# A second PSUM bank for the rounded copies, and new instruction orders on VectorE and ScalarE, in layer 0 of a two-layer graph network

## What is computed

```python
agg = jax.ops.segment_sum(x[src], dst, num_segments=N)
h = (1.0 + eps) * x + agg
h = jax.nn.relu(batch_norm(h @ W1 + b1, g1, be1))   # W1: 512 x 1024, layer 0
h = h @ W2 + b2                                     # W2: 1024 x 512
...
# layer 1: where(indeg > 0, agg, x) @ W.T + b, relu, batch norm
```

## Time and profile before

| | |
|---|---|
| median of 3 runs | 2925.01 us (2919.75 to 2929.12) |
| the profiled execution's own time | 2951.29 us |
| its span | 2949.5 us |
| mean granted TensorE clock | 0.902 |
| busy, share of the span | PE 81%, PEld 54%, DVE 49%, ACT 35%, POOL 53% |
| layer 0, from the second pair's start to the 25th's | 93.6 to 1218.2 us |

### The profile page before, as it was taken

The page is one execution under the profiler, slowest core; times in us unless marked ns, Lnnn a source line. Parts: engine busy times, 40 slices in busy tenths (PEclk is TensorE's granted clock), DMA queues, the critical chain, the costliest instruction groups (busy, mean ns, idle before and its releaser), DMA issues. The chain is left out here.

```text
span 2949.5 us, 42174 instructions
## 1 busy us (share of the span) xinstructions
PE 2402.7 (81%) x9711; PEld 1593.3 (54%) x9712; DVE 1447.7 (49%) x2269; ACT 1022.3 (35%) x1776; POOL 1555.5 (53%) x1731
## 2 busy tenths in 40 slices
PE   4888888887888887889997487978898787878885
PEld 2555555555555555578886354544444454445454
DVE  4444444444444444453336555545554454555448
ACT  2444444444444444455555311111111111111126
POOL 6565656666566666300002466666666666666633
PEclk9989989999999999999997698988898898988886
DMA  7666666666666676433326666665666666666668
GB/s 244 191 207 199 201 191 203 193 208 203 192 205 201 195 205 203 136 105 98 97 83 175 232 190 186 185 192 167 190 185 186 185 187 190 181 194 180 185 179 270
DMA packets 164329, 545.46 MB, mean 185 GB/s; under 512 B 30979, under 2 KB 34906, under 8 KB 159522
## 3 DMA queue, kind: packets, MB, share of 16 engines
q0 software_dynamic: 125120, 410.09, 48.3%
q1 hardware_dynamic: 17608, 78.33, 8.7%
q10 hardware_dynamic: 21544, 56.48, 5.6%
HBM read 493.18 MB, written 51.60 MB: 185 GB/s over the span
## 5 line engine op out<-in xcount | busy, mean ns | idle before, releaser
L848 PE MATMUL psum<-ring,select 128*125 x2400 | 1272.5, 632 | 71.7 <-issue 66.2
L595 POOL DMA_INDIRECT ring<-x_in,src_t x782 | 740.6, 947 | 479.1 <-issue 213.2
L595 POOL DMA_INDIRECT ring<-x_d,src_t x782 | 755.8, 967 | 430.0 <-issue 215.8
L962 ACT ACTIVATE rows_hi<-ring 128x512 fp32r x606 | 376.4, 630 | 851.4 <-issue 505.9
L884 PE MATMUL psum<-sumsT_hi,w_hi 128*128 128x250 f32 x1248 | 580.7, 465 | 97.6 <-DVE sumsT_lo L721 65.9
L848 PEld LDWEIGHTS psum<-ring,select 128*125 128x125 f32 x2400 | 433.6, 200 | 271.9 <-issue 238.6
L698 DVE TENSOR_TENSOR rows_lo<-ring,psum 128x512 fp32r<-128x512 f32 x404 | 277.5, 687 | 599.8 <-issue 323.8
L833 PE MATMUL psum<-rows_hi,select_r 128*125 128x512 f32 x600 | 372.2, 620 | 65.0 <-DVE rows_lo L698 36.3
L884 PEld LDWEIGHTS psum<-sumsT_hi,w_hi 128*128 128x128 f32 x1248 | 248.8, 199 | 277.8 <-issue 201.5
L884 PE MATMUL psum<-sumsT_lo,w_hi 128*128 128x250 f32 x1248 | 360.8, 289 | 40.2 <-issue 38.7
L884 PE MATMUL psum<-sumsT_hi,w_lo 128*128 128x250 f32 x1248 | 361.8, 290 | 37.5 <-issue 37.5
(11 more groups left out here) (191 smaller groups left out, 2495.2 us busy)
## 6 DMA issues: line engine op xcount, KB each, us to landing
hidden_d<-of_layer ACTq DMA_DIRECT2D x25, 1000.0 KB
act_f<-hidden_d SPq DMA_DIRECT2D x24, 1000.0 KB
ring<-x_in,src_t POOLq DMA_INDIRECT x782
ring<-x_d,src_t POOLq DMA_INDIRECT x782
sums<-x_in ACTq DMA_DIRECT2D x50, 224.0 KB
sums<-x_d ACTq DMA_DIRECT2D x50, 224.0 KB
rows_r<-x_in SPq DMA_DIRECT2D x6, 1120.0 KB
x_d<-rows_r SPq DMA_DIRECT2D x6, 1120.0 KB
```

Of the source, the lines that this page charges most:

```text
L595: nc.gpsimd.indirect_dma_start(slot(c % S), None, table, bass.IndirectOffsetOnAxis(ap=index_of(c), axis=0)).then_inc(gathered[c % S], 16)
L848: whole = nc.tensor.matmul(agg(h), select[h][:, WHOLE_AT.index(p), :], of_chunk(pe, first, place), start=False, stop=n + 1 == WINDOW, skip ...
L962: high = nc.scalar.activation(rows_hi[:, k, :], of_chunk(act, first, SPLIT_AT[k]), ACT.Copy)
```

## The change

In layer 0 the second rounded copy goes alternately to banks 5 and 3, so that ScalarE waits for the subtraction of the row before the last one (`AHEAD = 2`), and only between its two writes. Bank 3 is freed by turning the sums in two halves through bank 2: four transposes behind place 7 as before, and the other four behind place 11, once VectorE has read the first half. The orders on ScalarE and VectorE are written anew: `EARLY` is 2 in place of 4; the last two statistics of a pair go into the next iteration (`late_statistics`); the product's banks are emptied at other points between the split rows; the pieces of the product start at place 16 in place of 14. In layer 1 the order stays.

```diff
-    PIECE_AT = {14 + n * 22 // 15 if layer == 0 else 16 + n: n for n in range(PIECES)}
+    TURN_REST_AT = 11 if layer == 0 else None
+    PIECE_AT = {16 + n * 20 // 15 if layer == 0 else 16 + n: n for n in range(PIECES)}
...
-    EARLY = 4 if layer == 0 else 2
+    LATE = 6 if layer == 0 else KM
+    EARLY = 2
+    TURNS = 2 if layer == 0 else 1
...
-        turn_ps = m.banks(2, 4)
+        turn_ps = [m.bank(2), m.bank(2 if layer == 0 else 3)]
-        high_ps = m.bank(5)
-        AHEAD = 1 if layer == 0 else 0
+        high_ps = [m.bank(5), m.bank(3)]
+        AHEAD = 2 if layer == 0 else 0
...
+                def late_statistics(v, pair):
+                    for k in range(LATE, KM):
+                        dve.wait_ge(out_done, KM * v + k + 1)
+                        last = nc.vector.bn_stats(stats[:, k, bass.ds(pair * 6, 6)], hidden[:, k, :])
+                    last.then_inc(stats_done, 1)
...
                         read_sums(v, tiles(pair, 1), 1)
+                        if layer == 0:
+                            low_rows(v, 0, first, EARLY, 4)
+                            late_statistics(v, dve.snap(earlier, min_val=0, max_val=z.PAIRS - 1))
...
-                            low_rows(v, 0, first, 4, 6)
-                            low_part(v)
-                            low_rows(v, 0, first, 6, SPLIT)
+                            low_rows(v, 0, first, 4, 5)
+                            low_part(v, (0,))
+                            low_rows(v, 0, first, 5, 7)
+                            low_part(v, (1,))
+                            low_rows(v, 0, first, 7, SPLIT)
                             selection(v, 1, tiles(i, 1), second)
-                            low_rows(v, 1, second, 0, 6)
+                            low_rows(v, 1, second, 0, 3)
                             read_sums(v, tiles(i, 0), 0)
+                            low_rows(v, 1, second, 3, 4)
...
+                def turn_rest(job):
+                    pe.wait_ge(lo_done, 2 * job + 2)
+                    turn_half(1)
...
                         act.wait_ge(split_used, SPLIT * (2 * v + h) + k + 1)
-                        if layer == 0:
-                            act.wait_ge(split_lo, SPLIT * (2 * v + h) + k + 1)
                         act.wait_ge(landed, begin + (SPLIT_AT[k] + 1))
                         high = nc.scalar.activation(rows_hi[:, k, :], of_chunk(act, first, SPLIT_AT[k]), ACT.Copy)
                         if layer == 0:
-                            high = nc.scalar.activation(high_ps.bitcast(F32R), of_chunk(act, first, SPLIT_AT[k]),
+                            act.wait_ge(split_lo, SPLIT * (2 * v + h) + k + 1)
+                            nc.scalar.sem_inc(waited, 1)
+                            high = nc.scalar.activation(high_ps[k % 2].bitcast(F32R), of_chunk(act, first, SPLIT_AT[k]),
                                                         ACT.Copy)
...
-                            high_rows(following_begin, v + 1, 0, following, 0, 2)
-                            read_product(v, pair, 2)
-                            high_rows(following_begin, v + 1, 0, following, 2, EARLY)
+                            high_rows(following_begin, v + 1, 0, following, 0, 1)
                             read_product(v, pair, 3)
+                            high_rows(following_begin, v + 1, 0, following, 1, EARLY)
```

More of the change, by code:

```diff
@@ L644, in _ @@
                 nc.vector.sem_inc(lo_done, 1)
-                nc.vector.sem_inc(stats_done, 1)
+                if layer == 1:
+                    nc.vector.sem_inc(stats_done, 1)
                 if layer == 0:
                     nc.vector.sem_inc(split_lo, AHEAD)
+                    nc.vector.memset(hidden[:, LATE:, :], 0.0).then_inc(out_done, OUT_START)
                 if layer == 0:
@@ L652, in _ @@
                 dve.reg_mov(before, 0)
+                earlier = dve.alloc_register(f"dve_earlier{layer}")
+                dve.reg_mov(earlier, 0)
                 nc.vector.memset(m.bank(1), 0.0).then_inc(agg_zeroed, 1)
@@ L714, in read_sums, with low_part @@
                                                    ALU.add).then_inc(sums_done[h], 1)
-                def low_part(job):
+                def low_part(job, halves=(0, 1)):
                     dve.wait_ge(product_done, HALVES * job + 1)
-                    for b in range(2):
+                    for b in halves:
                         dve.wait_ge(hi_done, 2 * job + b + 1)
@@ L775, in _ @@
                         if layer == 0:
+                            low_rows(v, 1, second, 4, 6)
+                            statistics(v, pair, 0, 2)
                             low_rows(v, 1, second, 6, SPLIT)
[L777 to L781, removed]
+                            statistics(v, pair, 2, LATE)
+                            low_rows(v + 1, 0, following, 0, EARLY)
                         else:
@@ L785, in _ @@
                         dve.reg_mov(first0, following)
+                        dve.reg_mov(earlier, pair)
                         dve.reg_mov(before, i)
@@ L788, in _ @@
                 read_sums(uses, tiles(z.PAIRS - 1, 1), 1)
+                if layer == 0:
+                    late_statistics(uses, dve.snap(earlier, min_val=0, max_val=z.PAIRS - 1))
                 low_part(uses)
@@ L818, in clear, with scatter @@
                                      skip_group_check=True)
-                def scatter(i, v, g, tile, h, between):
+                def scatter(i, v, g, tile, h, between, later):
                     tile_use = pe.snap(2 * v + h)
@@ L829, in scatter @@
                             between()
+                        if n == TURN_REST_AT:
+                            later()
                         if p in SPLIT_AT:
@@ L862, in turn, with turn_half @@
                         clear(m.psum[0:z.NT, bass.ds(at, 1)])
[L863 removed]
+                    if layer == 0:
+                        turn_half(0)
+                    else:
+                        turn_half(0, then=lambda: turn_half(1))
+                def turn_rest(job):
+                    pe.wait_ge(lo_done, 2 * job + 2)
+                    turn_half(1)
+                def turn_half(b, then=None):
+                    for k in range(b * z.KD // 2, (b + 1) * z.KD // 2):
                         for h in range(2):
                             at = (k % (z.KD // 2)) * z.W + h * z.NT
[L866 removed]
+                            last = nc.tensor.transpose(turn_ps[b][:, at:at + z.NT],
                                                        sums[h][:, k * P:(k + 1) * P], m.ident[0:z.NT, 0:z.NT])
[L868 removed]
+                    if then is None:
+                        last.then_inc(turned, 1)
+                    else:
+                        then()
                 parts = [(w, s, k) for k in range(z.KD) for w, s in ((w_hi, sumsT_hi), (w_hi, sumsT_lo), (w_lo, sumsT_hi))]
@@ L912, in _ @@
                 turn(uses)
+                if layer == 0:
+                    turn_rest(uses)
                 pe.wait_ge(product_out, HALVES * uses + 1)
```

47 lines of the change are left out of this document (28 added, 19 removed).

## The result

The changed kernel takes 2965.64 us (median of four runs, 2952.79 to 2988.16), the kernel before beside it 2927.07: a ratio of 1.0146, 95% interval 1.0118 to 1.0175. So it is slightly slower, and clear of the noise, where 2823 us was forecast; that is outside the range. The profiled execution took 2952.79 us, its span is 2951.0. In three later comparisons the ratio was 1.0189, 1.0164 and 1.0128.

The account below looks back on a forecast made before the run. The ScalarE-VectorE loop was taken as the bound, then TensorE: 37.0 + 1.7 + 4.25 + 1.7 = 44.65 us a pair instead of 48.9, 102 us over 24 pairs, giving 2823 us, range 2783 to 2867.

Parts of the forecast that it names:

- The loop and the bank: Split rows between ScalarE and VectorE: 2.31 us each falls to 1.12 with a second bank; TensorE's 37.0 then binds.
- the walk: Step-by-step sum of engine times through one layer 0 pair: 44.2 us before; after, 37.0 of TensorE work plus 1.7 waiting.
- the clock: TensorE's granted clock of 0.93 in layer 0: 0 to 3.4 us a pair of lost work, taken as 1.7.
- The pair's start: TensorE waits behind the last emptying: 1.0 us at split row k = 1, 0.7 at k = 2, 1.7 instead of 3.2.
- ScalarE late: Rival at the pair's start: emptying, store and loop's end take longer with one row ahead; pair 50, 2951 us, chance 0.09.
- The halves of the turn: Sums turned in two halves sharing a bank: other places cover copy and difference, so the second half's wait is zero.
- The 41 us: Cost by the skill's rule if the turn's two halves in one bank don't overlap: 1.7 x 24; the forecast took nothing.
- What the walk doesn't have: Layer 0 stretches of slow rows without releaser, 2.0 to 4.25 us a pair, taken as 4.25; plus the clock, 1.7.
- no change: Rival: something the loop only follows, as the gathers' slots, holds layer 0's pairs; time stays 2925 us, chance 0.06.
- the thin lead: Part of the weaker rival: k = 1, 2 and second half turn wait longer; pair 46.5 to 48.5, 2867 to 2915, chance 0.14.

Follow-up runs that it names:

- early3: Changed kernel with rows 0, 1 and 2 of the next pair made ahead of the last emptying, instead of row 0 only: 2974.01 us (1.0066).
- after_narrow: Changed kernel with layer 0's gathers bringing 256 columns instead of 512: 2527.97 us (0.96) where the kernel before took 2633.07; later 2998.04 (1.0160) beside 2949.19.

## Why the prediction was wrong

**The loop and the bank: right, the size partly by luck.** The 2.31 us were the bound of the chain, and they became 1.04. With half the gathers the changed kernel has 38.5 us a pair, against 37.0 + 1.7 = 38.7 in the walk. The kernel before has 42.6, and there the walk gave 44.2, so 1.6 too much. It seemed confirmed by the shortest pair, 44.65, but that pair still held some of what the walk leaves out. That the gain with half the gathers, 97.8 us, comes close to the forecast's 102 is luck: 1.6 too much in one place stood against 1.7 for the clock in another.

**The pair's start: right in itself, and too long.** With half the gathers TensorE waits 0.74 us at k = 1 and 0.35 at k = 2, where the walk had 1.0 and 0.7. With all gathers it is 94.2 / 23 = 4.1 us at the split rows, because the last emptying comes late. The rival "ScalarE late" named this place, 2951 us and a slower kernel; but early3 shows that it passes the time on and doesn't make it.

**The halves of the turn: right.** 1.1 us in all, and nothing with half the gathers; other matmuls stand between the two halves. The Trainium skill's Perfetto Trace Analysis, section Matmuls, wants independent groups in different banks. The 41 us that were put beside that rule, for halves that share a bank, do not show in the trace.

**What the walk doesn't have: here the prediction failed.** I took the stretches of the earlier trace rows as a cost that comes from outside, "their size is the mean pair less the shortest", 4.25 us a pair before as after, and 1.7 for the clock beside it: 5.95. Measured as the pair with all gathers less the pair with half of them, the two together are 48.9 - 42.6 = 6.3 us before, but 49.4 - 38.5 = 10.9 after. The windows divide the 10.9. TensorE's matmuls are busy 948.62 / 23 = 41.2 us a pair instead of 859.60 / 23 = 37.4, at a granted clock of 0.92 instead of 1.00 (2.4 GHz): 3.9 us, above even the 3.4 at which the prediction bounded the clock. TensorE's idle time is 8.2 us instead of 1.1: 7.1 us. So the cost is not a constant that a shorter chain leaves alone. It comes with gathers issued close together, and wherever these run on a chip with slow rows, the pair is at 47 to 50.5 us: in both kernels, under the old orders, with three early rows, and in layer 1.

How a shorter chain raises the cost from 6.3 to 10.9 is not shown. It is not by longer runs of gathers, nor by more slow rows: the kernel before makes 7.9 gathers to a run and 191 slow rows, the changed one 6.7 and 117. It may be that before, part of each stretch fell into TensorE's waits for the chain, and now no such waits are left; no run tells.

**The rival "no change"** named the true kind of cause, something that the loop only follows, with 0.06. I set the 2.31 us of the earlier trace rows against it, which show that there was a loop, not that it alone set the time. The Trainium skill's TensorE: Matmul & The Clock Gate, section HAM oscillation, tells of a kernel with long waits for transfers, in whose reordered version double-buffered PSUM gave no further gain. Here the second bank gave none either on three of the four chips that were noted, though the bytes of the transfers had no part in it.

**Why 1.3 to 1.9% slower, and not the same,** is shown in part only. On one chip three rows ahead of the last emptying gave 1.0066 (1.0043 to 1.0089) and the changed kernel, in another comparison, 1.0128 (1.0092 to 1.0165); so the thin lead seems to cost some 0.5%. The rest stays open, as does why the bank under the old orders is at 1.0098.

**Open, too:** whether the chip itself or what else runs on it makes the difference; what in the gather slows the sequencers; and the changed kernel on the chip without slow rows, which it never met. That it takes 0.96 there is argued from after_narrow (0.9598), whose halved bytes made no difference elsewhere. No version that makes all its gathers beat both kernels where slow rows are.

## What to carry to other kernels

Look at a stage that has the same supplier but another chain before you price a shorter one: layer 1, where ScalarE is busy for 7.5 us a pair instead of 22 and no row waits for two handoffs, took 47.1 us for the same 31.3 gathers, 1.50 us each beside layer 0's 1.56; that stood in the trace of before. Idle time without a releaser is not a constant to be added: halve the supplier's work in both kernels and see whether it goes. And time a change on more than one chip before its sign is believed: this one gains 98 us when half the gathers are gone, and loses 1.3 to 1.9% in all four comparisons of the whole kernel, each on a chip with slow rows.

## What the runs showed of the hardware

The same program took 2633 us on one chip and 2927 to 2956 us on the others. The difference lies in the gather stages (a pair of layer 1 took 40.0 us there and 47.1 elsewhere), and goes with slow instructions on the sequencers of TensorE, ScalarE, VectorE and SyncE. On the other chips single instructions take 0.7 us and more while GpSimd issues indirect gathers 1.25 us apart: 111 to 221 slow rows in layer 0, most of them from the sixth gather of a run on. With breaks after every fourth gather there are 3, with plain transfers at 253 GB/s one, and on the one chip there are none. A gather's bytes play no part: 1.0160 with half of them, 1.0189 with all.
